# Last layer's attention: additive masks by accumulating DMAs from GpSimd instead of GpSimd additions, and GpSimd subtracting the maxima of all heads

## The reference, cut to what matters

```python
def attention(q, k, v, mask):
    scores = jnp.einsum('bhqd,bhkd->bhqk', q, k) / jnp.sqrt(jnp.float32(HD))
    scores = scores * mask - 10000.0 * (1.0 - mask)
    probs = jax.nn.softmax(scores, axis=-1)
    return jnp.einsum('bhqk,bhkd->bhqd', probs, v)
...
ctx = merge_heads(attention(split_heads(q), split_heads(k), split_heads(v), ltor_mask))
x = hidden_states + ctx @ w_ao + b_ao
...
ctx = merge_heads(attention(split_heads(q), split_heads(k), split_heads(v), cross_mask))
x = x + ctx @ w_co + b_co
```

## Time and profile before

| | |
|---|---|
| time, median of 3 runs | 1385.88 us (1384.08 to 1386.36) |
| the profiled execution's own time | 1384.41 us |
| its span in the profile | 1382.6 us |
| PE busy | 1277.6 us, 92% |
| DVE busy | 828.4 us, 60% |
| ACT busy | 740.8 us, 54% |
| POOL busy | 540.8 us, 39% |
| DMA issued by POOL | none |

### The profile page before, as it was taken

How to read it: one execution, slowest core, us unless ns; L and a number is a source line. 1 busy time by engine, 2 the same in 40 slices (tenths; PEclk the granted TensorE clock), 3 DMA queues, 4 the chain that set the end, 5 groups by cost and what they waited for, 6 DMA issues and landing times.

```text
span 1382.6 us, 24470 instructions
## 1 busy us (share of the span) xinstructions
PE 1277.6 (92%) x8912; PEld 1008.2 (73%) x8912; DVE 828.4 (60%) x1900; ACT 740.8 (54%) x2040; POOL 540.8 (39%) x571
## 2 busy tenths in 40 slices
PE   6999999999988988999999999999998986787788
PEld 5777777777644556899999889999985654645555
DVE  4666666766547985666666776666673029638620
ACT  4665555555545884555554655455544147647631
POOL 3554444544339983331121413121202039439420
PEclk9999999999998999999999999999999998997989
DMA  6101011010010003020111111020001010000000
GB/s 254 49 26 51 26 37 40 26 51 26 5 64 0 2 1 131 18 69 32 47 32 47 33 45 58 20 69 14 12 1 61 0 61 1 1 16 1 1 8 23
DMA packets 15525, 50.44 MB, mean 36 GB/s; under 512 B 1840, under 2 KB 5296, under 8 KB 14384
## 3 DMA queue, kind: packets, MB, share of 16 engines
q1 hardware_dynamic: 15408, 48.87, 10.6%
HBM read 47.82 MB, written 1.05 MB: 35 GB/s over the span
## 4 chain that ended last, share of the span: by engine, by line
PE 81%; DVE 12%; ACT 3%; issue 2%; POOL 1%; DMA 0%; SPq 0%; DVEq 0%; POOLq 0%
PE pS L1648 12%; PE acc L315 6%; PE pT L1676 6%; PE acc L1728 6%; PE pC L378 5%; PE pT L365 5%; PE pS L348 4%; PE pS L1690 4%; PE acc L334 4%; PE pC L1713 4%; DVE stats L1299 3%; PE acc L921 3%; PE acc L390 3%; PE pT L1452 2%; PE heads_transposed L1136 2%
## 5 line engine op out<-in xcount | busy, mean ns | idle before, releaser
L1648 PE MATMUL pS<-split_sources,split_pair_weights 128*128 128x512 f32 x768 | 211.9, 411 | 5.8 <-issue 4.3
L665 POOL TENSOR_TENSOR probs<-probs,stats 128x512 f32<-128x512 f32 x128 | 130.6, 1042 | 182.4 <-DVE stats L543 182.4
L486 ACT ACTIVATE probs<-pS,stats 128x256 f32<-128x256 f32 x256 | 118.1, 473 | 136.2 <-DVE stats L538 136.2
L1648 PEld LDWEIGHTS pS<-split_sources,split_pair_weights 128*128 128x128 f32 x768 | 135.8, 190 | 30.7 <-issue 6.6
L1825 ACT ACTIVATE probsT<-pT 128x256 f32<-128x256 f32 x128 | 49.3, 385 | 197.0 <-PE pT L1701 197.0
L1728 PE MATMUL acc<-l_wo_parts,l_ctx_parts 128*128 128x256 f32 x768 | 121.9, 295 | 1.0 <-DVE l_ctx_parts L1897 1.0
L538 DVE TENSOR_REDUCE stats<-pS 128x2 f32<-128x512 f32 x128 | 82.4, 686 | 62.0 <-PE pS L348 61.9
L1676 PEld LDWEIGHTS pT<-l_wv_parts,split_sources 128*128 128x128 f32 x756 | 106.9, 188 | 14.2 <-issue 2.2
L1676 PE MATMUL pT<-l_wv_parts,split_sources 128*128 128x256 f32 x756 | 110.6, 281 | 2.1 <-issue 2.1
L1951 POOL TENSOR_TENSOR split_pair_weights<-weights_a,split_pair_weights 128x1024 fp32r<-128x1024 f32 x16 | 38.1, 2382 | 170.0 <-ACT split_pair_weights L1789 170.0
L315 PE MATMUL acc<-split_sources,split_pair_weights 128*128 128x512 f32 x372 | 101.9, 409 | 1.0 <-POOL split_pair_weights L652 0.7
(11 more groups left out here) (206 smaller groups left out, 2976.4 us busy)
## 6 DMA issues: line engine op xcount, KB each, us to landing
weights_a<-in_l_w SPq DMA_DIRECT2D x16, 768.5 KB, 4.3
weights_a<-in_l_w SPq DMA_DIRECT2D x16, 768.0 KB, 5.8
value_bias_rows<-in_l_bv SPq DMA_DIRECT2D x16, 256.0 KB, 4.4
weights_b<-in_l_wo SPq DMA_DIRECT2D x16, 256.0 KB, 2.7
w_fc<-in_l_w SPq DMA_DIRECT2D x4, 1024.0 KB, 6.0
bias_rows<-in_rows SPq DMA_DIRECT2D x1, 1536.0 KB, 13.4
x_residual<-in_x_dbl SPq DMA_DIRECT2D x2, 512.0 KB, 7.0
masked_scores<-in_ctx_dbl SPq DMA_DIRECT2D x2, 512.0 KB, 7.9
```

Of the source, the lines that this page charges most:

```text
L486: a = e.activation(self.E[:, n % 4, h, it, :], self.S[h][:, it, :], ACT.Exp, bias=self.st[:, 1, n % 4, h, it:it + 1], accum_out=self.st[:, ...
L665: e.tensor_tensor(self.E[:, n % 4, h, :, :], self.E[:, n % 4, h, :, :], self.st[:, 3, n % 4, h, :].unsqueeze(2).broadcast_to([P, 2, D]), A ...
L1648: mm = e.matmul(bank[:, :], self.w_qk[i % 2][kw][:, 1 - which, c, h * P:h * P + P], g.split[:, which, ks, c, half * HALF:half * HALF + HAL ...
```

## The change

`add_masks` no longer computes: for each part (1024 columns, eight heads) POOL issues one DMA whose destination is the scaled scores and whose source is the additive mask, repeated eight times, with `accum_op=ALU.add`. The maxima wait for the DMA's semaphore, one of four. `shift` now covers all 16 heads in four instructions; the exponentials are two of 1024 columns without bias. The second half of the transposed probabilities is copied out by ACT instead of DVE. On DVE both scalings of batch `t` now come first in the iteration, and then `normalise` and the two maxima.

```diff
-            scores_shifted=R if multiply else 4 * R, exp_ready=2 * R, transposed_in_bank=2 * R,
+            scores_shifted=4 * R, exp_ready=2 * R, transposed_in_bank=2 * R,
...
+        self.masked = [g.counts("small_heads", **{f"masks_added_{i}": 8 * R if multiply else 0})[0] for i in range(4)]
...
-        def add_masks(r, c):
+        def add_masks(r, part):
             b = 0 if self.one_mask else self.unit(r)[0]
-            wait(e, self.scaled, 2 * r + c // 2 + 1)
-            s = self.heads(self.sm[r % 3])[:, 4 * c:4 * c + 4, :]
-            e.tensor_tensor(s, s, g.amask[:, b, :].unsqueeze(1).broadcast_to([P, 4, P]), ALU.add)\
-                .then_inc(self.masked.sem, 1)
+            wait(e, self.scaled, 2 * r + part + 1)
+            e.dma_start(self.heads(self.sm[r % 3])[:, 8 * part:8 * part + 8, :],
+                        g.amask[:, b, :].unsqueeze(1).broadcast_to([P, 8, P]), accum_op=ALU.add)\
+                .then_inc(self.masked[2 * (r % 2) + part].sem, 16)
 
         def shift(r, c):
-            wait(e, self.nmax, self.parts * (r + 1))
+            wait(e, self.nmax, 2 * r + c // 2 + 1 if self.multiply else r + 1)
...
-        if self.multiply:
-            for r in range(self.R + 1):
-                if r < self.R:
-                    add_masks(r, 0)
-                    add_masks(r, 1)
-                if r >= 1:
-                    shift(r - 1, 3)
-                if r < self.R:
-                    add_masks(r, 2)
-                    add_masks(r, 3)
...
+        for r in range(self.R):
+            if self.multiply:
+                add_masks(r, 0)
+                add_masks(r, 1)
+                for k in range(r - 1, r + r // (self.R - 1)):
+                    for c in range(4 if k >= 0 else 0):
+                        shift(k, c)
+                continue
...
         def exps(r, half):
             s = self.sm[r % 3]
             whole = slice(1024 * half, 1024 * half + 1024)
-            if not self.multiply:
-                wait(e, self.shifted, 4 * r + 2 * half + 2)
-                a = e.activation(s[:, whole], s[:, whole], ACT.Exp)
-            else:
-                wait(e, self.nmax, 2 * r + half + 1)
-                for n in range(8 * half, 8 * half + (8, 4)[half]):
-                    at = slice(n * P, n * P + P)
-                    a = e.activation(s[:, at], s[:, at], ACT.Exp, bias=self.nm[r % 3][:, n:n + 1])
-                if half == 1:
-                    wait(e, self.shifted, r + 1)
-                    a = e.activation(s[:, 1536:2048], s[:, 1536:2048], ACT.Exp)
-            a.then_inc(self.exp.sem, 1)
+            wait(e, self.shifted, 4 * r + 2 * half + 2)
+            e.activation(s[:, whole], s[:, whole], ACT.Exp).then_inc(self.exp.sem, 1)
...
                 if 0 <= t - 2 < self.R:
                     evacuate_t(t - 2, 0)
+                    evacuate_t(t - 2, 1)
...
-                wait(e, self.masked, 4 * r + 2 * part + 2)
+                wait(e, self.masked[2 * (r % 2) + part], 16 * (r // 2 + 1))
...
             if self.multiply:
-                if 0 <= t - 3 < self.R:
-                    evacuate_t(t - 3)
+                if t < self.R:
+                    scale_and_mask(t, 0)
+                    scale_and_mask(t, 1)
                 if 0 <= t - 4 < self.R:
                     normalise(t - 4)
                 if 0 <= t - 1 < self.R:
                     maxes(t - 1, 0)
-                if t < self.R:
-                    scale_and_mask(t, 0)
-                if 0 <= t - 1 < self.R:
                     maxes(t - 1, 1)
-                if t < self.R:
-                    scale_and_mask(t, 1)
```

More of the change, by code:

```diff
@@ L1005, in __init__ @@
         H = self.parts
-        (self.keys, self.s_full, self.scaled, self.masked, self.nmax, self.shifted, self.exp,
+        (self.keys, self.s_full, self.scaled, self.nmax, self.shifted, self.exp,
          self.t_full, self.pt0, self.pt1, self.c_full, self.ot, self.tb_full, self.rec, self.ctx,
@@ L1009, in __init__ @@
             "small_heads", keys_masked=0 if multiply else R, scores_in_bank=R, scores_scaled=H * R,
-            scores_masked=4 * R if multiply else 0, negmax_ready=H * R,
-            scores_shifted=R if multiply else 4 * R, exp_ready=2 * R, transposed_in_bank=2 * R,
+            negmax_ready=H * R,
+            scores_shifted=4 * R, exp_ready=2 * R, transposed_in_bank=2 * R,
             probsT_half0_ready=R, probsT_half1_ready=R, contextT_in_bank=R, contextT_ready=R,
@@ L1080, in pool @@
             self.cross.pool_first(e)
-        if self.multiply:
-            for r in range(self.R + 1):
-                if r < self.R:
-                    add_masks(r, 0)
-                    add_masks(r, 1)
-                if r >= 1:
-                    shift(r - 1, 3)
-                if r < self.R:
-                    add_masks(r, 2)
-                    add_masks(r, 3)
-        else:
-            for r in range(self.R):
-                if r + 2 < self.R:
-                    mask_keys(r + 2)
-                for c in range(4):
-                    shift(r, c)
+        for r in range(self.R):
[6 more added lines that the diff above has]
+                continue
+            if r + 2 < self.R:
+                mask_keys(r + 2)
+            for c in range(4):
+                shift(r, c)
         if self.cross:
@@ L1301, in maxes @@
                             negate=True).then_inc(self.nmax.sem, 1)
-        def evacuate_t(r):
-            wait(e, self.t_full, 2 * r + 2)
-            if r >= 2:
-                wait(e, self.c_full, r - 1)
-            e.tensor_copy(self.PT[r % 2][:, 1024:2048], self.bT[:, :, :].rearrange("p n t -> p (n t)"))\
-                .then_inc(self.pt1.sem, 1)
         def normalise(r):
```

1 line of the change is left out of this document (removed).

## The result

The changed kernel takes **1439.19 us** (median of 4 runs, 1435.24 to 1439.8) against 1385.14 us for the kernel before in the same comparison: a ratio of 1.0384, 95% interval 1.0366 to 1.0402. It is 54 us slower. The profiled execution took 1438.8 us. Forecast were 1422 us with a range of 1405 to 1500.

The account below looks back on a forecast made before the run. DVE was taken to bound the middle before, a closed loop of 9.9 us after. Filling 6.4, middle 8.0 and draining 3.4 make 17.8 us per attention, plus 1.0 for the clock: 37.6 for two, from 1384.4 to 1422 us, range 1405 to 1500.

Parts of the forecast that it names:

- The loop: Iterations 5 to 7, around PE, ACT and DVE: ten steps and four hand-overs make 9.9 us per batch, without a DMA.
- g: POOL's time to issue one accumulating DMA: taken as 1.5 us; POOL stays under 9.9 us per batch until 2.9.
- The transfer: One accumulating DMA's passage through the queue: 3.3 us as two passes, bounds 1.6 and 4.9.
- Filling: First scores to the end of iteration 4: 32.2 us after against 25.8 before, 6.4 more.
- 1.0 for the clock: Added per attention because TensorE's clock was at 0.50 in the second attention's filling, and filling gets longer.
- The schedule: All instructions of one attention in code order, one engine at a time; for before it gave 70.0 us, measured 71.1.
- The clock: Rival: in iterations 5 to 7 PE's clock falls, its steps take 1.8 times as long, 1482 us; chance 0.05.
- Draining: End of iteration 7 to the last addition: 25.9 us, 3.4 more, from iterations 8 and 9 and ACT's second copy.
- middle: Iterations 5 to 7 of each attention: 3 x 9.9 = 29.7 us, 8.0 more than before.
- likeliest case: Iterations of 9.9 us with the DMAs covered: chance 0.62, its own range 1405 to 1449 us.
- The DMA-bound case: Rival: descriptors or transfers become the bound; 1484 us at 6 us per transfer, 1558 at 8.3; chance 0.27.
- The freed DVE decides: Rival: the loop does not close, a batch costs DVE's 5.5 us in place of 6.6, 1367 us; chance 0.04.

Follow-up runs that it names:

- the kernels with added work: Changed kernel with PE doing the first half of the transposes twice, in every iteration: 1437.93 us; in iterations 3 to 6 only: 1438.86 us.
- DMAs alone: Kernel before with only the additive masks by DMA, its order, copy and exponentials kept: 1444.99 us, ratio 1.0434.
- both edits undone: Changed kernel with the second copy back on DVE and normalising ahead of the scalings, DMAs kept: 1423.03 us, ratio 1.0284.

## Why the prediction was right, and where its sizes were off

**The loop: right.** Forecast was an iteration of 9.9 us out of ten terms and four hand-overs. Measured are 9.9 us in iterations 6 and 7 of both attentions, with the waits that were named (back transposes for the context copy, normalised transposes for the product). It is there without a DMA, and it shrinks where it is opened: to 8.1 by the copy back on DVE or by the context copy early, where the clock doesn't drop, to 8.0 to 8.9 by normalising first, and to 6.3 to 6.8 by normalising first and the context copy early together, with no DMAs. DVE was to idle "some 40%": of 9.9 us it has 4.2 of waits in brackets.

**g: a little small.** 1.5 us was taken, 1.54 to 2.24 measured, median 1.64 and 1.85, far under the 2.9 at which POOL would decide.

**The transfer: too small by 0.3 to 0.7 us, and inside its bounds.** Taken was 3.3 us as two passes of 26 ns per packet; measured 3.6 to 4.0. Two passes fit the 4 KB packet (310 ns against 2 x 147 of the earlier trace rows); what failed is the line drawn down to 512 B, which gave 2 x 26 = 52 ns where 75 were measured. (Since packets overlap, the 65 packets of an engine, 4.9 us one after another, pass in 3.8.) A line through the two accumulating kinds is 41 ns plus 67 ns per KB (235 ns over 3.5 KB): a fixed part five times the 8 ns of the plain copies. The plain packets were measured in an almost idle queue and these in a full one, so how much of the 41 ns is the adding and how much the crowding is open. By the Trainium skill (DMA: Bandwidth & Descriptors, Anatomy of one DMA), 2.0 us plus bytes over 436 GB/s, a part would land in 3.2 us. The runs disagree: the quickest landing was 7.1 us at 512 B and 4.6 at 4 KB, both counted from the start of POOL's issue. The Trainium skill also says (DMA: Bandwidth & Descriptors, Why small descriptors are slow (HBM only)) that transfers from SBUF to SBUF don't suffer from small descriptors. Here the same bytes took 82.3% of 95 us in 512 B runs and 44.6% of 100 in 4 KB runs, so for accumulating DMAs written by GpSimd the measurement decides against it.

**Filling: 6.4 and 1.0 for the clock, where 11.1 and 8.4 were measured.** The schedule had the two DMAs of batch 0 landing at 8.6 and 11.9 us. DVE's maxima start on them at 10.5 and 15.3 us (1150.53 and 1155.32, from 1140.02). That is 1.9 us more for the first: POOL begins to issue it 0.8 us later than taken (1143.20), issues for 1.78 us, and it lands 5.5 us behind the end of its issue, where 4.7 was taken. The second loses another 1.5. The schedule let it have the queue for itself, but POOL has issued the DMAs of the next batch from 1147.41 on, and by 1155.3 the queue has moved 1.29 MB, where the two parts of batch 0 are 1.05 MB. With 4 KB runs filling is 31.0, with none 30.7 and 29.6: the DMAs hold 6.9 and 8.0 us of the growth, and of the first's 6.6 come from the 512 B runs. The other 4.2 and 0.4 us need no DMA. Most of the difference between these two is the clock before: it had risen by the second half of the first batch's transposes in the first attention (1.06 us) and not in the second (1.94), while after the change it is low there in both (1.94). The prediction had its 1.0 for the clock from the second attention alone.

**The clock: the rival was wrong as a whole and right in pieces; 1.0 us per attention was too little.** The clock did not stay at its 1.2 GHz level (0.50) in the loop, but it drops there, and again in draining. What that costs stands in PE's timeline of iteration 5 beside iteration 6: context 1.94 against 1.08, output 1.65 against 1.13.

```profile
1184.17 0.60 PE L1172 MATMUL heads_output<-consts,v 128*128 128x128 f32 x2 [2.17 <-DVE v L1297]
1184.71 1.94 PE L1148 MATMUL heads_context<-probsT,big 128*32 128x128 f32 x32
1186.57 1.65 PE L1178 MATMUL heads_output<-weights_a,value_bias_rows 128*128 128x256 f32 x4
```

Iteration 5 is 11.5 and 12.9 us instead of 9.9, iteration 8 is 8.4 in both instead of the 7.1 forecast, and the last output of the first attention takes 2.08 us instead of 1.13: 3.8 and 4.3 us from drops of the clock behind filling. The prediction argued from draining before, where PE was as thinly busy at 1.00; one such stretch was no guide. That thin work *causes* the drops is supported (more work on PE moved them), not settled: the kernels with added work lost the same time elsewhere. What does settle the drops stays open.

**Draining: 3.4 forecast, 5.6 and 4.6 measured.** 1.3 of each is the clock in iteration 8, and 1.0 of the first the clock in its last output. What is left is 3.3 in both, about what was forecast: the longer iterations 8 and 9, and ACT's context copy behind the second copy, which costs some 2 us after the last transposes by the run that moves it (12.0 instead of 14.0, with the last output slow in both, 1.91 and 2.08).

**The sum.** Forecast 37.6 for both attentions, measured 52.8. Of the 8.2 and 7.0 us missing per attention, middle and draining hold 4.5 and 6.0, of which 3.8 and 4.3 are the clock's; the rest there, 0.8 and 1.8, is that the schedule had 21.7 us for the middle before, where 20.9 and 19.9 were measured. Filling holds 3.7 and 1.0. Another 1.6 us lie outside. So the mis-sized steps are the clock's term and the landing in filling. The forecast of 1422 was 17 us low. That the time is in the range, and even in the likeliest case's own 1405 to 1449, is in part luck: its upper end came from transfers of 4.9 us, which were not measured, and not from a clock that drops in the middle, which was. Filling grew by 11.1 us, not far under the 12 that would have spoken against the prediction.

**The rivals.** The DMA-bound case did not come with this order: in iterations 5 to 7 of the first attention DVE waited for a DMA twice, 4.3 us, both times ahead of the first iteration of 9.9. It is real in the other orders (DMAs alone, normalising first, both edits undone), where DVE waits for landings in most iterations. "The freed DVE decides" had the loop lacking 3.3 us; with the loop open and no DMAs the iteration was still 6.3 to 6.8, not 5.5, so most of that gain does not exist in PE's order as it is.

No version tried beats the kernel before; the nearest, without the additive masks, is at 1.0053. Not tried: 4 KB runs in the second attention, which need the eightfold mask of every batch.

## What to carry to other kernels

When work moves between engines, walk once around the in-order queues with the durations of the trace before adding up busy time: here relieving the busiest engine by 1.13 us per batch closed a loop of 9.9 us where 6.60 had been the bound. A DMA in place of an engine's operation is priced by its landing where nothing covers it (filling, or an order in which the next issue stands behind the wait), and by no more than its transfer where a batch of other work lies between; in this order even that did not show. Undo parts one by one and also do them one by one: their costs, 45 and 59 us, came to 54 together, and neither difference alone would have told that. And compare iterations only at the same granted clock: undoing the copy read as no gain in the middle (9.7 us) until one iteration without a drop showed 8.1.

## What the runs showed of the hardware that was not expected

- An accumulating DMA from SBUF to SBUF, 512 KB in 1024 runs: 1.54 to 2.24 us of POOL's time to issue, 1040 packets of 75 ns that overlap, mostly 131 to 147 GB/s, landing after 7.1 us at best and 9.3 in the median.
- The same bytes in 4 KB source runs: 0.86 to 1.17 us to issue, 144 packets of 310 ns, about 210 GB/s, landing after 4.6 and 6.0 us.
- In these loops the granted clock was mostly 1.00, with drops to 0.50 (1185 to 1187 us in the changed kernel) that lengthened one iteration of 9.9 us by 1.6 to 3.0 us. With the copy back on DVE each full iteration of the first attention had one. Work added to PE moved the drops and did not remove them.
